# Two attention layers and an MLP in one kernel: another order on SyncE's DMA queue, and layer 2's norm chain in four parts

## Reference

```python
def multilora(x, W, A, B):                       # one adapter per sequence, rank 16
    return x @ W.T + (x @ A.T) @ B.T
Q, K, V = heads(multilora(x, Wq..)), heads(multilora(x, Wk..)), heads(multilora(x, Wv..))
Q, K = rope(Q), rope(K)
a = softmax(causal(Q @ K.T / sqrt(32))) @ V
x = layernorm(x + multilora(merge(a), Wo, Ao, Bo))
# second part
n = rmsnorm(x, ln1_w);  attn = attention(n, Wq2, Wk2, Wv2, Wo2)     # no rope
mod = 0.1 * tanh(attn @ A2)
h = rmsnorm(x, ln2_w)
gate = silu(h @ W_in.T + mod * (h @ A2) @ B2)
out = layernorm(x + x_residual_mlp),  x_residual_mlp = (gate * (h @ W_up.T)) @ W_down.T
```

## Time and profile before

| | |
|---|---|
| median of 3 runs | 2922.37 us (2917.73 to 2923.05) |
| the profiled execution | 2919.17 us, span 2917.3 us |
| mean granted TensorE clock | 0.961 of full |
| busy, PE / DVE / ACT / POOL | 2639.0 / 1580.4 / 1335.8 / 645.8 us |
| layer 1, layer 2, layer 3 (from the exponentials' first and last) | about 74 to 842, 930 to 1745, 1797 to 2917 us |

### The profile page before, as it was taken

How to read it: one execution, slowest core, us unless ns; L and a number is a source line. 1 busy time by engine, 2 the same in 40 slices (tenths; PEclk the granted TensorE clock), 3 DMA queues, 4 the chain that set the end, 5 groups by cost and what they waited for, 6 DMA issues and landing times. The chain is left out here.

```text
span 2917.3 us, 40940 instructions
## 1 busy us (share of the span) xinstructions
PE 2639.0 (90%) x13584; PEld 2029.4 (70%) x13584; DVE 1580.4 (54%) x4310; ACT 1335.8 (46%) x2755; POOL 645.8 (22%) x528
## 2 busy tenths in 40 slices
PE   5989988998748999899999884999999999999998
PEld 4767766776536666666666653888888888888886
DVE  3777777777635777776786763322222333333333
ACT  2776777767633666666666663211111221111111
POOL 5455555555321122222212111000000000000000
PEclk8999999999878999999999987999999999999999
DMA  5455555555625545455445534211111221111100
GB/s 139 96 140 135 141 121 136 132 131 118 153 85 125 120 101 137 109 111 132 112 107 130 109 64 143 88 45 45 44 44 44 77 91 46 45 45 44 44 29 29
DMA packets 173898, 276.44 MB, mean 95 GB/s; under 512 B 29204, under 2 KB 53524, under 8 KB 173076
## 3 DMA queue, kind: packets, MB, share of 16 engines
q1 hardware_dynamic: 170772, 260.58, 37.0%
q0 software_dynamic: 2304, 12.58, 1.3%
q10 hardware_dynamic: 640, 1.05, 0.1%
HBM read 97.04 MB, written 42.99 MB: 48 GB/s over the span
## 5 line engine op out<-in xcount | busy, mean ns | idle before, releaser
L2233 DVE TENSOR_TENSOR c_product<-c_up_ps,c_gate 128x512 f32<-128x512 f32 x128 | 88.6, 692 | 654.5 <-PE c_up_ps L2299 654.4
L2287 PE MATMUL c_gate_ps<-c_h_split,c_w_split 128*128 128x512 f32 x1536 | 381.2, 397 | 22.1 <-DVE c_w_split L2185 22.1
L2271 PE MATMUL c_down_ps<-c_w_split,c_product_split 128*128 128x512 f32 x1536 | 379.3, 396 | 0.0
L2299 PE MATMUL c_up_ps<-c_h_split,c_w_split 128*128 128x512 f32 x1536 | 378.2, 394 | 0.0
L2287 PEld LDWEIGHTS c_gate_ps<-c_h_split,c_w_split 128*128 128x128 f32 x1536 | 289.6, 189 | 94.4 <-issue 23.8
L2299 PEld LDWEIGHTS c_up_ps<-c_h_split,c_w_split 128*128 128x128 f32 x1536 | 288.1, 188 | 70.6
L2271 PEld LDWEIGHTS c_down_ps<-c_w_split,c_product_split 128*128 128x128 f32 x1536 | 288.4, 188 | 69.1
L2157 ACT ACTIVATE c_gate<-c_gate_ps 128x512 f32<-128x512 f32 x128 | 76.7, 599 | 494.2 <-PE c_gate_ps L2294 494.2
L280 ACT ACTIVATE b_prob_hi<-b_scores_t_ps 128x384 fp32r<-128x384 f32 (+1 forms) x384 | 201.1, 524 | 220.7 <-PE b_scores_t_ps L271 196.6
L288 DVE TENSOR_TENSOR a_prob_lo<-a_scores_t_ps,a_prob_hi 128x384 fp32r<-128x384 f32 (+1 forms) x384 | 225.7, 594 | 134.1 <-ACT a_scores_t_ps L281 132.5
L288 DVE TENSOR_TENSOR b_prob_lo<-b_scores_t_ps,b_prob_hi 128x384 fp32r<-128x384 f32 (+1 forms) x384 | 226.1, 594 | 124.1 <-ACT b_scores_t_ps L281 123.0
(11 more groups left out here) (206 smaller groups left out, 4776.7 us busy)
## 6 DMA issues: line engine op xcount, KB each, us to landing
a_q_stack<-a_q_split SPq DMA_DIRECT2D x192, 128.0 KB, 3.7
a_k_stack<-a_k_split SPq DMA_DIRECT2D x192, 128.0 KB, 3.7
b_q_stack<-b_q_split SPq DMA_DIRECT2D x192, 128.0 KB, 3.3
b_k_stack<-b_k_split SPq DMA_DIRECT2D x192, 128.0 KB, 3.6
c_h_stage<-h_t SPq DMA_DIRECT2D x16, 1024.0 KB, 6.2
c_res<-x SPq DMA_DIRECT2D x16, 1024.0 KB, 5.5
c_w_stage<-in_mlp_w POOLq DMA_DIRECT2D x16, 768.0 KB, 4.7
stage<-in_x_t SPq DMA_DIRECT2D x8, 1024.0 KB, 6.2
```

Of the source, the lines that this page charges most:

```text
L2233: dve.tensor_tensor(product[:, bank, :], up_ps[:, bank, :], gate[:, bank, :], ALU.mult).then_inc(product_done, 1)
L2271: mm = pe.matmul(down_ps[:, t, :], product_split[:, kt % 2, a, t * P:t * P + P], w_split[:, w, kt, 2 * KC * P:], start=(kt == 0 and i == 0 ...
L2287: pe.matmul(gate_ps[:, bank, :], w_split[:, w, ft, c * 2 * P:c * 2 * P + P], h_split[run.pair][:, a, c, :], start=(c == 0 and w == 0 and a ...
L2299: mm = pe.matmul(up_ps[:, bank, :], w_split[:, w, ft, c * 2 * P + P:(c + 1) * 2 * P], h_split[run.pair][:, a, c, :], start=(c == 0 and w = ...
```

## The change

In layer 1, SP's order in a step becomes: `send_b` (group 1), gather, load (group 0), `send_low` (group 1), first half of `spread` (out), stack pair 0, second half (in), store, stack pair 1. In layer 2, group 3 alone: first half, stack pair 0, second half. GpSimd's `merge` in layer 2 is cut in two, and the attention chunks and adapter of group 3 go between the parts. The low product of layer 1 is dealt to slots 1 to 4 as 2, 3, 3 and 4 matmuls in place of 3 each. `norm_factors` is cut: variances ahead of lo part 9, start and first round behind it, two rounds behind lo part 10 in slot 11.

```diff
+LOW_ITEMS = (range(0, 2), range(2, 5), range(5, 8), range(8, 12))
...
-            def spread(b, g):
+            def spread_out(b, g):
                 n = number(b, g)
                 sp.wait_ge(inverted, n + 1)
                 sp.dma_start(sums_hbm.rearrange("h (c n) -> (h c) n", c=TT), inverse[:, :]).then_inc(inverse_out, 16)
+
+            def spread_in(b, g):
+                n = number(b, g)
                 sp.wait_ge(inverse_out, n * 16 + 16)
                 sp.dma_start(inverse_all[:, :], sums_hbm.rearrange("(o h) n -> o h n", o=1).broadcast_to(
                     [HD, GH, SEQ])).then_inc(inverse_in, 16)
...
                 last = is_last(b)
+                first = isinstance(b, int) and b == 0 and g == 0
+                if g == 1 and not last:
+                    send_b(b + 1)
+                if not first:
+                    gather(*group(b, g, -1))
                 if g == 0 and not last:
                     load(b + 1)
-                first = isinstance(b, int) and b == 0 and g == 0
-                if not first:
-                    gather(*group(b, g, -1))
                 if g == 1 and not last:
-                    send_b(b + 1)
                     send_low(b + 1)
                 if not first:
-                    spread(*group(b, g, -1))
+                    spread_out(*group(b, g, -1))
                 if not (last and g >= 2):
                     stack_send(sp, at, *group(b, g, 2), 0)
                 if not first:
+                    spread_in(*group(b, g, -1))
                     store(*group(b, g, -1))
                 if not (last and g >= 2):
                     stack_send(sp, at, *group(b, g, 2), 1)
...
-                        low(b + 1, share(3 * KC, LOW_SLOTS[1] - LOW_SLOTS[0], slot - LOW_SLOTS[0]))
+                        low(b + 1, LOW_ITEMS[slot - LOW_SLOTS[0]])
...
                 if not first:
-                    spread(*group(b, g, -1))
+                    spread_out(*group(b, g, -1))
+                if g < 3 and not first:
+                    spread_in(*group(b, g, -1))
                 if g == 2 and has(b, 2):
                     load(b + 2)
                 if g == 0 and not last:
                     load_x(b + 1)
                 if not (last and g >= 2):
                     stack_send(sp, at, *group(b, g, 2), 0)
+                if g == 3:
+                    spread_in(*group(b, g, -1))
                 if g == 3 and has(b, 2):
                     send_b(b + 2)
                     send_low(b + 2)
...
                 pool.tensor_tensor(sum_hi[:, :], sum_hi[:, :], sum_lo[:, :], ALU.add).then_inc(merged, 1)
+
+            def weigh(b, g):
+                n = number(b, g)
                 pool.wait_ge(merged, n + 1)
                 pool.wait_ge(inverse_in, n * 16 + 16)
...
+                    if not (isinstance(b, int) and b == 0 and g == 0):
+                        merge(*group(b, g, -1))
                     if g == 3 and has(b, 2):
                         for c in range(KC):
                             attn_chunk(b + 2, c)
                         adapter(b + 2)
                     if not (isinstance(b, int) and b == 0 and g == 0):
-                        merge(*group(b, g, -1))
+                        weigh(*group(b, g, -1))
...
+                    if g == 1 and slot == 10 and not last:
+                        variances(b + 1)
                     if slot > 0:
                         lo_unit(dve, at, b, g, slot - 1)
...
                         if slot == 10:
-                            norm_factors(b + 1)
+                            root_start(b + 1)
+                            root_round(b + 1, 0)
                         if slot == 11:
+                            for i in range(1, 3):
+                                root_round(b + 1, i)
                             normalise_tile(b + 1, 0)
                             normalise_tile(b + 1, 1)
```

More of the change, by code:

```diff
@@ L614, in _ @@
             gather(BATCH - 1, GROUPS - 1)
-            spread(BATCH - 1, GROUPS - 1)
+            spread_out(BATCH - 1, GROUPS - 1)
+            spread_in(BATCH - 1, GROUPS - 1)
             store(BATCH - 1, GROUPS - 1)
@@ L1121, in rsqrt, with rsqrt_start @@
 def rsqrt(dve, step, done, out, x, t):
+    rsqrt_start(dve, step, done, out, x, t)
+    for i in range(3):
+        rsqrt_round(dve, step, done, out, x, t, i)
+def rsqrt_start(dve, step, done, out, x, t):
     dve.tensor_scalar(t.bitcast(I32), x.bitcast(I32), 1, None, ALU.logical_shift_right).then_inc(step, 1)
@@ L1125, in rsqrt, with rsqrt_round @@
     dve.tensor_scalar(out.bitcast(I32), t.bitcast(I32), -1.0, RSQRT_MAGIC, ALU.mult, ALU.add).then_inc(step, 1)
[L1126 to L1132, removed]
+def rsqrt_round(dve, step, done, out, x, t, i):
+    dve.wait_ge(step, done + 2 + 3 * i)
+    dve.tensor_tensor(t, out, out, ALU.mult).then_inc(step, 1)
+    dve.wait_ge(step, done + 3 + 3 * i)
+    dve.scalar_tensor_tensor(out=t, in0=t, scalar=-0.5, in1=x, op0=ALU.mult, op1=ALU.mult).then_inc(step, 1)
+    dve.wait_ge(step, done + 4 + 3 * i)
+    dve.scalar_tensor_tensor(out=out, in0=t, scalar=1.5, in1=out, op0=ALU.add, op1=ALU.mult).then_inc(step, 1)
 RSQRT_STEPS = 11
@@ L1630, in add_residual, with variances @@
                 dve.bn_stats(stats[:, t, :], res[:, t, :]).then_inc(stats_done, 1)
-            def norm_factors(b):
+            def variances(b):
                 done = b * LN_STEPS
@@ L1745, in _ @@
                 add_residual(0, t)
-            norm_factors(0)
+            variances(0)
+            root_start(0)
+            for i in range(3):
+                root_round(0, i)
             for t in range(TT):
```

9 lines of the change are left out of this document (7 added, 2 removed).

## The result

The changed kernel takes 2976.44 us (median of 4 runs, 2971.34 to 2982.49), the kernel before 2922.71 (4 runs, 2917.73 to 2923.90) on the same chip. The ratio is 1.0188, with a 95% interval of 1.0164 to 1.0211: slower by 1.9%, 53.7 us. The forecast was slower, 2953 with 2936 to 2978. That the time still fell inside the range is in part luck, since the room above 2953 was meant for other causes.

A forecast was written before the change was run, and what follows sets the result against it. SP's in-order queue was taken to set layer 1's turn. Turns +31, last batch +6 and norm chain -6 gave +31 us on the profiled 2919.2, so 2950, or 2953 against the runs' median; range 2936 to 2978.

The forecast's parts named there:

- SP's queue sets the turn: Layer 1: the loop through SP's queue, copy to copy of head 0, has no slack and closes to 20.88 us.
- The rival that SP isn't the bound: Layer 1: the store's wait stays hidden and TensorE's named waits go, giving 2887 us; chance 0.05.
- the shorter turn: Rival, layer 1: the broadcast lands 1.0 us earlier than 3.60, over 27 turns, giving 2926 us; chance 0.04.
- Out to store 9.44: Layer 1, SP's queue: from the sums' issue to the store grows from 6.27 to 9.44 us, +3.17 a turn.
- four turns are 23.8 + 26.0 + 26.2 + 23.8 = 99.8 us, 24.95 a step: Layer 1: the four groups' turns, against 23.8 us a step before; +1.15 a step, +31 over 27 turns.
- No penalty, so I keep 3.60.: Layer 1: broadcast issue to multiply stays 3.60 us behind six stack transfers, judged by the gather's 5.33 and 5.54.
- The 4.40 from the copy to the sums' issue: Layer 1: time from head 0's copy to the sums going out, kept at 4.40 us in a plain turn.
- The 2.4 for `send_low`: Layer 1, group 1: send_low stays ahead of spread_out and adds 2.4 us to one turn, making 26.2.
- Later transfers make it worse: Rival, layer 1: broadcast, gathers or pair 1 come later; +1 us a turn gives 2980; worse than 2978 had chance 0.11.
- send_b: Layer 1, group 1: its three issues ahead of the gather add 2.2 us to one turn, making 26.0.
- Gathers ahead of loads: Layer 1, group 0: the load's four instructions leave one turn in four, which becomes a plain 23.8 us.
- Batch 0 and the last batch: Layer 1: batch 0 has three turns at +1.15 us; later layer 2 weights behind pair 1 cost the last batch +6.

The follow-up runs named there:

- experiment 1: Changed kernel with layer 1's broadcast directly behind the sums again, ahead of stack pair 0; 2895.64 us, ratio 0.9903 to the kernel before.
- experiment 2: Kernel before with only layer 1's stack pair 0 put between the sums and the broadcast; 2992.58 us, ratio 1.0237.
- experiment 4: Changed kernel with the store behind stack pair 1 and the product written over inverse_all, pair 0 staying in the middle; 2886.36 us, ratio 0.9874.
- experiment 11: Changed kernel with send_b behind the gather in group 1 again; 2965.56 us, ratio 1.0165 to the kernel before.
- experiment 6: Experiment 1 with the load ahead of the gather in group 0 again; 2914.16 us, ratio 0.9972 to the kernel before.
- experiment 3: Kernel before with only layer 2's norm chain cut in four parts; 2913.74 us, ratio 0.9972.
- experiment 7: Experiment 1 with send_b behind the gather in group 1 again; 2899.33 us, ratio 0.9919 to the kernel before.
- experiment 9: Changed kernel with layer 1's broadcast issued between the q and k transfers of stack pair 0; 2920.86 us, ratio 0.9997 to the kernel before.
- experiment 8: Experiment 4 with SP's and GpSimd's old order in layer 2's group 3; 2888.13 us, ratio 0.9881 to the kernel before.
- experiment 10: Experiment 4 plus two layer 2 normalise tiles behind lo part 11, with layer 1's broadcast ahead of stack pair 0, store last; 2893.45 us, ratio 0.9897.

## Why the prediction was right, and where its size was off

**SP's queue sets the turn: right.** Experiments 1, 2 and 4 show it from three sides. The rival that SP isn't the bound fell with the 113.6 us of waits, and so did the shorter turn: the broadcast took 4.02 us to the multiply in the turn shown and not 1.0 less than 3.60. The Trainium skill ("DMA: Bandwidth & Descriptors", Anatomy of one DMA) gives 2.0 us plus bytes over 436 GB/s, there for transfers that GpSimd issues, an estimate of 2.6 us for these 256 KB. This broadcast is issued by SyncE, and the traces have 3.55 and 3.77 us from issue to landing, on average before and after; they decide. The page's advice under Rules for kernel authors, to issue early, compute, and wait late, is what experiment 4 does: SP issues the broadcast, then pair 1, and only then waits for the multiply that needs the broadcast. The runs agree: 90 us faster than the changed kernel.

**Out to store 9.44: right,** 9.63 in that turn. On average over batches 1 to 6 this way went from 6.84 to 9.86 us, 3.02 more where 3.17 was forecast.

**The size of a turn: too small.** The step that was mis-sized is "four turns are 23.8 + 26.0 + 26.2 + 23.8 = 99.8 us, 24.95 a step". From copy to copy of head 0, over batches 1 to 6, the turns from groups 0, 1, 2 and 3 are 26.37, 27.39, 24.59 and 24.13 on average: 102.5, or 25.62 a step. Before they were 24.01, 25.75, 21.27 and 23.83, or 23.72. The rise is 1.90 a turn and not 1.15; over 24 turns 45.7 us instead of 27.6. Terms that were kept as they stood before grew:

- "No penalty, so I keep 3.60." The broadcast behind six stack transfers took 3.77 us on average from issue to landing, where it was 3.55, so 0.2 a turn. To the multiply's start it was 3.68 on average before and 3.91 after. The comparison with the gather was made of two single turns; for the gather it holds (5.2 to 5.5 us to the copy in all four groups, for 5.33).
- The 4.40 from the copy to the sums' issue. From the copy to the reciprocal's end were 4.44 us on average before and 4.74 after: 5.33 in group 1 and 4.91 in group 2, but 4.37 in groups 0 and 3. In group 2 the sums' issue comes 4.94 us after the copy for 4.40.
- The 2.4 for `send_low` in group 1, whose turn exceeds its sum most (27.39 for 26.2). `send_low` waits for the lo part of the low product, which stands right behind the reciprocal on VectorE, so it is late by the same. From the copy to the sums' issue are 7.83 us on average where the sum has 6.8 and the trace of before 7.04.

The wait for the copy isn't enough to make the reciprocal late: in 16 of the 24 turns it ends 4.4 to 4.5 us after the copy, although TensorE waits for the copy in most of them too. The other 8 are turns in which TensorE's clock was halved for 3.1 to 4.0 of the 4 us behind the copy, against 2.1 at most in the 16. The last section shows two turns. The clock falls in or behind the long waits, so I read this as a loss that feeds itself; no run holds the clock and keeps the waits, so that step is argued.

This is much of the rival "Later transfers make it worse", which had a chance of 0.11 with the cases above 2978: the broadcast lands later and pair 1 comes too late for the scores of slot 5, but the gathers don't land later.

**send_b:** its turn was put at 26.0 and took 26.37. Seven batches x 2.2 us are 15; experiment 11 gives 10.9.

**Gathers ahead of loads:** the turn into group 0 was put at 23.8 and took 24.13, hardly more than the 23.83 before. The gain was inside the sum and is spent there; freed from the store's wait it shows as 18.5 us (experiment 6).

**Batch 0 and the last batch:** +5.9 where three turns gave 3.5. The last batch had +5.8 up to its last copy of head 0, where 6 was forecast for it, and 3 more behind that, up to layer 2's first exponential.

**TensorE's waits: half right.** The one for the copy did grow, to 53.8 and not to over 60. The one for pair 0 went, all 14.4 us of it. But the 11.5 us after are a new wait, for pair 1 in slot 5: pair 1 stands behind the store's wait. The prediction had this only as a rival ("pair 1 comes too late for the scores of slot 5") and its sum put nothing down for it; what it costs beside the wait for the copy, which comes next, no run separates.

**Layer 2: right.** Part 10's stall is gone, part 11's is there with 1.4 to 1.8 us, and the gain is 7.3 us (experiment 3: 4.4 in the profile, 8 by the medians) for 6 forecast. One profile tells little here: in those of the changed kernel and experiments 1, 4, 6, 7, 9 and 11, whose layer 2 is the same code, this stretch takes 859.6 to 868.3 us, 864.0 on average; in those of before and experiment 2, with the old code, 866.9 and 873.9. The waits for parts 10 and 11 are the firmer figure, 5.5 us less in seven batches. Group 3 at 0 holds within what the runs can tell, some 6 us (experiment 8).

**Sum.** In the profiled executions the change cost 52.2 us, forecast 31. Of the 21 missing, 18 are the turns of batches 1 to 6, 2 those of batch 0 and nearly 3 the last batch; layers 2 and 3 give 2 back. The range's upper end doesn't quite follow from its own parts: 2953 + 22 + 5 are 2980, not 2978.

**What looks like the same and isn't.** In experiments 1 and 4 the reciprocal ends 5.0 to 5.5 us after the copy in all six turns of group 0, with no fall of the clock there. In these turns the copy came early: ScalarE idled 0.4 us at most for the gather before it, where it had idled 2.1 to 3.9 in the kernel before. In experiment 2 all twelve turns with 4.9 us or more have a fall of the clock for 1.9 to 4.0 of the 4 us behind the copy.

**Open.** What makes the clock fall after one wait and not after another isn't settled by these runs. The sums of experiment 9 are made of single turns. By averages over batches 1 to 6 the way from the sums' issue to the store is 6.78 us in experiment 1, 7.98 in experiment 9 and 9.86 in the changed kernel: 27 x 3.08 are 83 us for the 81 measured, and 27 x 1.20 are 32 for 25. Most of the difference in the larger step was the choice of the turn; in the smaller one it is the turns from groups 0 and 1, which hardly grew.

## What to carry to other kernels

In a queue that issues in order, what matters of a moved transfer is less its own place than which waiting instruction now stands in front of the others: write down the loop through the queue, check that it closes to the turn seen, and then put last what nobody in the loop needs, unless its wait is hidden already, as in experiment 10. A wait that is hidden by work that then moves elsewhere comes back, here nearly whole. And take the other terms of the loop from many turns, since a later turn lengthens them too.

## What the runs showed of the hardware

TensorE's clock took part in the loss. In batches 1 to 6 of layer 1 the granted clock fell to half 11 times in the changed kernel, 10 of them in groups 1 and 2, each time within TensorE's wait for the copy or up to 1.5 us behind it. It fell 13 times in experiment 2, 3 times before, twice in experiment 1 and never in experiment 4. The waits right ahead were not all long: before they were 1.8 to 2.7 us. Two stretches of the changed kernel, at the same place of a step (columns as in the earlier trace rows), with the value product behind the wait and the reciprocal:

```profile
313.00:316.40 3.40, 2.57 (x11) 2.00 (x12) 1.45 (x6) 3.31 (x7) 3.32 (x3) 0.79 0.02 7
414.80:418.20 3.40, 2.55 (x9) 1.77 (x10) 0.56 (x1) 3.24 (x7) 3.31 (x3) 0.50 0.00 0
```

```profile
313.83 0.42 PE L305 MATMUL a_pv_ps<-a_prob_hi,a_value 128*65 128x512 f32 x1 [3.11 <-ACT a_pv_raw L317]
...
415.65 0.66 PE L305 MATMUL a_pv_ps<-a_prob_hi,a_value 128*65 128x512 f32 x1 [4.07 <-ACT a_pv_raw L317]
```

```profile
316.68 0.93 DVE L893 RECIPROCAL a_inverse<-a_sums 16x128 f32<-16x128 f32 x1
...
419.46 0.94 DVE L893 RECIPROCAL a_inverse<-a_sums 16x128 f32<-16x128 f32 x1
```

After 3.11 us of waiting the product takes 0.42 us; the stretch's 0.79 is a mean, 1.00 up to 314.9 and 0.50 from 315.1, so that the clock fell behind the product. After 4.07 us the whole stretch has 0.50, which is the lower of its two levels, 1.2 of 2.4 GHz, and the same product takes 0.66. The reciprocal starts 2.85 us after the product in the first and 3.81 in the second, since the score maxima ahead of it on VectorE wait for the slower matmuls. 8 of the 24 turns have such a late reciprocal, 5.5 us from the copy to its end in place of 4.4.

The broadcast's time from issue to landing, in the 24 steps of batches 1 to 6, in the kernel before, the changed kernel and experiment 4:

```profile
DMA to landing us min/median/max: 3.1/3.6/3.8
```

```profile
DMA to landing us min/median/max: 3.0/3.9/4.4
```

```profile
DMA to landing us min/median/max: 3.8/4.7/5.7
```

Its median is 3.6 us with six stack transfers right behind it, 3.9 with six right ahead of it, and 4.7 with six on either side. This is one shape, 256 KB, and experiment 4 is the fastest of the three in spite of it.
